# Router matmul as three rounded passes, with PSUM-bank alignment, routing totals and a few early and late steps rearranged

## The reference

```
h = rmsnorm(xn) * scale                       # 8192 tokens x 128
q, k, v = h @ wq, h @ wk, h @ wv              # 16 heads of 64
attn = softmax(q k^T / 8) v @ w_out + b_out   # per sequence of 512, fp32
z = silu(xn @ rw1 + rb1) @ rw2 + rb2          # router: 128 -> 512 -> 8
top 2 of 8 experts, softmax over the two
moe = sum_e weight_e * (silu(xn @ w1[e] + b1[e]) @ w2[e] + b2[e])
out = x + attn + moe
```

## Time and profile before

| what | value |
|---|---|
| median of 3 runs | 1897.01 us (1896.87 to 1897.79) |
| the profiled execution | 1897.01 us, span 1895.1 us |
| TensorE clock granted | 0.996 of full |
| PE busy | 1835.2 us (97%) |
| VectorE busy | 1625.8 us (86%) |
| ScalarE busy | 1198.8 us (63%) |
| chain that ended last | PE 55%, ACT 21%, DVE 14%, issue 8%, SPq 1%, DMA 1% |

### The profile page before, as it was taken

The page is one execution under the profiler, slowest core; times in us unless marked ns, Lnnn a source line. Parts: engine busy times, 40 slices in busy tenths (PEclk is TensorE's granted clock), DMA queues, the critical chain, the costliest instruction groups (busy, mean ns, idle before and its releaser), DMA issues.

```text
span 1895.1 us, 74351 instructions
## 1 busy us (share of the span) xinstructions
PE 1835.2 (97%) x32434; PEld 1149.5 (61%) x32434; DVE 1625.8 (86%) x2297; ACT 1198.8 (63%) x2969; POOL 711.9 (38%) x623
## 2 busy tenths in 40 slices
PE   8999999999999999998899999999999999999997
PEld 5555555555555555555566666666666666666655
DVE  5999999999999999989788888888888888888885
ACT  6666766666666666664567575666666666666563
POOL 3244654434444445432023234324324333333152
PEclk9999999999999999999999999999999999999999
DMA  3133322111111111111434434333333333333342
GB/s 90 27 82 109 97 94 57 42 48 37 47 38 47 48 48 48 29 42 44 116 74 78 90 72 89 78 84 77 90 72 65 93 69 84 72 83 78 78 76 53
DMA packets 154485, 130.13 MB, mean 69 GB/s; under 512 B 27664, under 2 KB 139024, under 8 KB 154128
## 3 DMA queue, kind: packets, MB, share of 16 engines
q1 hardware_dynamic: 123568, 104.65, 20.1%
q0 software_dynamic: 30592, 20.73, 8.3%
HBM read 93.15 MB, written 34.27 MB: 67 GB/s over the span
## 4 chain that ended last, share of the span: by engine, by line
PE 55%; ACT 21%; DVE 14%; issue 8%; SPq 1%; DMA 1%; ACTq 0%; DVEq 0%
PE pair L329 15%; ACT PR L910 13%; PE pair L310 12%; PE pair L469 7%; DVE NM L551 6%; PE pair L342 4%; PE pair L295 4%; DVE PT L559 3%; ACT ZT L992 3%; PE pair L385 3%; ACT ZZ L995 3%; PE pair L283 3%; PE pair L271 2%; DVE OT L568 2%; PE pair L239 1%
## 5 line engine op out<-in xcount | busy, mean ns | idle before, releaser
L910 ACT ACTIVATE PR<-pair,NM 128x512 f32<-128x512 f32 x1024 | 694.3, 696 | 544.1 <-DVE NM L551 543.7
L559 DVE STREAM_TRANSPOSE PT<-PR 128x1024 f32<-128x1024 f32 x512 | 631.7, 1240 | 109.5 <-ACT PR L910 96.3
L551 DVE TENSOR_REDUCE NM<-pair 128x2 f32<-128x1024 f32 x512 | 598.9, 1210 | 26.9 <-PE pair L310 26.6
L310 PE MATMUL pair<-KS,QS 64*32 64x512 f32 x8192 | 502.6, 596 | 18.1 <-ACT KS L886 10.2
L329 PE MATMUL pair<-PT,V 32*64 32x256 f32 x16384 | 479.4, 378 | 11.8 <-ACT ZZ L995 9.6
L1151 POOL DMA_INDIRECT out<-YS,IDW x156 | 248.9, 1596 | 611.3 <-DVE YS L828 387.5
L329 PEld LDWEIGHTS pair<-PT,V 32*64 32x64 f32 x16384 | 375.5, 131 | 165.5 <-issue 111.8
L310 PEld LDWEIGHTS pair<-KS,QS 64*32 64x32 f32 x8192 | 124.6, 106 | 259.2 <-issue 164.9
L910 ACT ACTIVATION_READ_ACCUMULATOR PR<-pair,NM 128x1 f32 x1024 | 218.3, 213 | 0.0
L992 ACT ACTIVATE ZT<-pair,BT 128x512 f32<-128x512 f32 x156 | 109.6, 703 | 115.4 <-PE pair L224 115.3
L1098 POOL TENSOR_TENSOR TH<-TH,HS 128x512 f32<-128x512 f32 x64 | 82.0, 1280 | 227.8 <-ACT HS L948 227.8
(11 more groups left out here) (121 smaller groups left out, 1688.3 us busy)
## 6 DMA issues: line engine op xcount, KB each, us to landing
RB<-l_rows SPq DMA_DIRECT2D x128, 256.0 KB, 4.4
E<-w_tab SPq DMA_DIRECT2D x39, 512.0 KB, 4.6
XG<-slots SPq DMA_DIRECT2D x39, 264.0 KB, 4.2
E<-in_w SPq DMA_DIRECT2D x39, 256.0 KB, 3.7
xin<-in_x SPq DMA_DIRECT2D x16, 256.0 KB, 3.0
XQ<-in_x SPq DMA_DIRECT2D x16, 256.0 KB, 3.2
l_rows<-RT SPq DMA_DIRECT2D x256, 2.0 KB
w_tab<-SPL SPq DMA_DIRECT2D x8, 512.0 KB, 2.7
```

Of the source, the lines that this page charges most:

```text
L310: m = pe.do.matmul(bank[2 * (s % 2) + r][32 * c:32 * c + 32, :], QS[rows, u % 2, c, at:at + 32], KS[rows, g % 2, c, :], start=True, stop=T ...
L551: dve.do.tensor_reduce(NM[:, step % 4], pairs[s % 2][:], AX.X, ALU.max, negate=True).then_inc(sem["dve_max"])
L559: dve.do.transpose(PT[:].rearrange("p c k q -> p (c k) q")[:, :, 32 * slot:32 * slot + 32], PR[:, step % PRB].rearrange("p r k -> p (r k)" ...
L910: act.do.activation(PR[:, step % PRB, r, :], bank[2 * (s % 2) + r], ACT.Exp, bias=NM[:, step % 4, r:r + 1], accum_out=RS[:, g % 2, r, at:a ...
```

## The change

1. The router's first layer: XT and R1 become pairs of fp32r tiles (high and low part). `router` calls `three` in place of one fp32 matmul. ScalarE writes the high part of XT; a new VectorE instruction, `split_x`, subtracts it from the bank to give the low part. It stands at the start of G = 8r, behind `denominators` and ahead of the first maximum. The bank of the transposed tokens now comes free with `split_x`, not with ScalarE's copy. At the start ScalarE and GpSimd split rw1 once, from a staging place in `acc`.
2. The tokens of sequence 0 are transposed before the loop, ahead of the first scores.
3. `ring.align` is removed.
4. `ends`, `starts` and `rows_of_tiles` follow `totals` directly at G = 131.
5. The denominators of the last unit are done at G = 256 like the others at their unit's end, behind VectorE's work for the last expert tile.
6. GpSimd no longer waits for VectorE's first rows before it starts on the routed rows of sequence 0.

```
-    def align(self):
-        self.used += -self.used % GH
...
             def turn_x(r):
-                free[bk] = sem["act_xTs"], r + 1
+                free[bk] = sem["dve_xTs"], r + 1
...
             def attending(G):
-                if k == 2:
-                    ring.align()
...
             def router(r, c):
+                w = [R1[:, k, c * P:(c + 1) * P] for k in range(2)]
+                m = [XT[:, k, :] for k in range(2)]
+                pe.wait_ge(sem["dve_xTs"], r + 1)
-                pe.do.matmul(bank[bk], R1[:, c * P:(c + 1) * P], XT[:], start=True, stop=True).then_inc(sem["pe_r1"])
+                three(pe, bank[bk], w, m).then_inc(sem["pe_r1"])
...
+            def split_x(r):
+                dve.wait_ge(sem["act_xTs"], r + 1)
+                dve.wait_ge(sem["pe_r1"], NC * r)
+                dve.do.tensor_tensor(XT[:, 1, :], bank[BANK["xT", r]], XT[:, 0, :], ALU.subtract).then_inc(sem["dve_xTs"])
...
             def between(G):
-                if G == EARLY * GB + 4:
-                    ends()
-                if G == EARLY * GB + 5:
-                    starts()
-                if G == EARLY * GB + 6:
-                    rows_of_tiles()
...
+            split_x(0)
             for G in range(TIMES + 8):
-                if k == 0 and 0 < u < UNITS:
+                if k == 0 and 0 < u <= UNITS:
                     denominators(u - 1)
+                turned(G)
...
-                if G == TIMES - 1:
-                    denominators(u)
                 experts(G)
...
+            def weight_high(name, src, dst, c, scale):
+                act.do.mul(dst[:, 0, s], src[:, s], scale).then_inc(sem["act_whi"])
+            weight_high("r1", r1_s, R1, 0, 1.0)
+            turn_x(0)
...
+            def weight_low_part(src, dst, c, rank):
+                pool.do.tensor_tensor(dst[:, 1, s], src[:, s], dst[:, 0, s], ALU.subtract).then_inc(sem["pool_wlo"])
-            pool.wait_ge(sem["dve_hc"], QT)
             routed_rows(0)
+            weight_low_part(r1_s, R1, 0, 1)
```

More of the change, by code:

```diff
@@ L41 @@
     pe_w2
[L42 removed]
+    dve_junk dve_one dve_ri0 dve_ones dve_bn dve_mv dve_var dve_hc dve_xTs dve_max dve_tr
     dve_OT dve_ri dve_rt dve_acc dve_sum dve_gate dve_pm dve_at dve_pk dve_row dve_to dve_wt dve_tot
     dve_xl dve_s dve_y dve_ys dve_rb1h dve_pm0 dve_hf
[L45 to L46 removed]
+    act_whi act_xTs act_V act_k act_q act_exp act_th act_hz act_tanh act_shi act_xh act_lgs act_zt act_zz
+    pool_half pool_pow pool_wlo pool_slo pool_hc pool_hr pool_xc pool_xr pool_tok pool_spare pool_tz pool_hs pool_bhalf
     pool_pad0 pool_pad pool_TOK pool_idw
@@ L147, in block_kernel @@
             XR = sb("XR", [P, 3, 2, QT, ROW], F32, routing)
-            XT = sb("XT", [P, S], F32, routing)
-            R1 = sb("R1", [P, HID], F32, routing)
+            XT = sb("XT", [P, 2, S], F32R, routing)
+            R1 = sb("R1", [P, 2, HID], F32R, routing)
             R2 = sb("R2", [P, NC, 32], F32, routing)
@@ L178, in block_kernel @@
         ov = out[0:T].rearrange("(b t p) d -> b p t d", t=QT, p=P)
+        r1_s = acc[:].rearrange("p t d -> p (t d)")
         full = [P, QT, D]
@@ L186, in x_in, with weight_low @@
             return sem[f"x_{b % 3}"], 16 * (b // 3 + 1)
+        def weight_low(name, c):
+            return sem["pool_wlo"], 1
         def place_of(g, s):
@@ L590, in project_out @@
                     dve.wait_ge(sem["pe_oT"], b)
+                    dve.wait_ge(sem["pool_wlo"], 1)
                     dve.do.tensor_scalar(dst, ps, BO[:], None, ALU.add).then_inc(sem["dve_acc"])
@@ L725, in place, with turned @@
                 dve.do.tensor_copy(junk[:, 2:3], junk[:, 0:1]).then_inc(sem["dve_gate"])
+            def turned(G):
+                r, h = divmod(G, 8)
+                if h == 0 and 0 < r < NB:
+                    split_x(r)
             def between(G):
@@ L760, in route @@
                     best(r)
-            lane = slice(0, 1)
-            nt, end, beg, cnt = (tot[:, k] for k in range(4))
-            ex, st, j = (tix[:, k] for k in range(3))
-            cmp = tic[:]
-            wide_e = [1, NT, E]
-            def totals():
+            def totals():
+                lane = slice(0, 1)
+                nt, end, beg, cnt = (tot[:, k] for k in range(4))
+                i = TILES[lane, :]
+                ex, st, j = (tix[:, k] for k in range(3))
+                cmp = tic[:]
+                wide_e = [1, NT, E]
                 dve.wait_ge(sem["pe_cnt"], 1)
                 dve.do.tensor_copy(cnt, bank[BANK[("cnt",)]][lane, 0:E]).then_inc(sem["dve_tot"])
-            def ends():
                 dve.wait_ge(sem["dve_tot"], 1)
@@ L782, in ends @@
                 dve.do.tensor_tensor_scan(end, ONES[lane, 0:E], nt, 0.0, ALU.mult, ALU.add).then_inc(sem["dve_tot"])
-            def starts():
-                i = TILES[lane, :]
                 dve.wait_ge(sem["dve_tot"], 6)
@@ L880, in _ @@
             act = Engine(eng)
+            def weight_high(name, src, dst, c, scale):
+                s = slice(c * 512, (c + 1) * 512)
+                act.wait_ge(sem[f"load_{name}{c}"], 16)
+                act.do.mul(dst[:, 0, s], src[:, s], scale).then_inc(sem["act_whi"])
             def keys(g, c):
@@ L896, in turn_x @@
                 act.wait_ge(sem["pe_r1"], NC * r)
-                act.do.copy(XT[:], bank[BANK["xT", r]]).then_inc(sem["act_xTs"])
+                act.do.copy(XT[:, 0, :], bank[BANK["xT", r]]).then_inc(sem["act_xTs"])
             def probs(g, s):
@@ L1036, in power @@
                 pool.do.tensor_tensor(sqo[:, r], sqi[:], HALF[:], ALU.pow).then_inc(sem["pool_pow"])
+            def weight_low_part(src, dst, c, rank):
+                s = slice(c * 512, (c + 1) * 512)
+                pool.wait_ge(sem["act_whi"], rank)
+                pool.do.tensor_tensor(dst[:, 1, s], src[:, s], dst[:, 0, s], ALU.subtract).then_inc(sem["pool_wlo"])
             def attention_rows(b):
@@ L1339, in _ @@
                 load(f"wv{c}", WV[:, cols], wv[:, cols])
-            load("r10", R1[:], rw1)
+            load("r10", r1_s, rw1)
             load_q(1)
```

13 lines of the change are left out of this document (2 added, 11 removed).

## The result

| | median | lowest to highest | ratio |
|---|---|---|---|
| before | 1896.91 us (5 runs) | 1894.68 to 1897.79 | |
| after | 1916.79 us (5 runs) | 1914.57 to 1919.28 | 1.0106, interval 1.0092 to 1.0121 |

The change costs 19.9 us. The prediction was 1901.2 with a range up to 1908.5: its sign was right, its size was a fifth of the truth, and the range did not hold the time. The profiled execution of the changed kernel took 1913.43 us, 16.4 us more than that of the kernel before; the traces hold that much of the 19.9 us.

What follows compares the result with a forecast made beforehand. TensorE and VectorE were both nearly full in the first half, TensorE set the second. First half +3.1, ring +4.0, boundary -4.3, start +0.6, tail +0.3 sum to +3.7: 1900.7 us, named 1901.2, range 1893 to 1908.5.

Steps and rivals of the forecast that it cites:

- How much of it shortens the span is limited by VectorE in stretch A: Router blocks: TensorE's saving of 0.34 us a pair counts up to VectorE's waits for scores, 5.9 us gained.
- stretch A: About 18 us around the router in each round of 8 G, where TensorE was said to set the pace.
- the second kind: Router places at G%16 = 10, 11, claimed to gain 0.51 us each, 8 times.
- the first kind: Router places at G%16 = 2, 3, claimed to gain at most 0.46 us each, booked 4 times.
- Split: New VectorE instruction ahead of a round's first maximum: 0.60 us paid in each of 15 rounds, +9.0 us.
- the bank rival: Bank held by the split delays weighted and later scores; a round costs 1.1 us, 1908.5 us in all; chance 0.20.
- Ring without alignment: Second half: queries wait for the second take-out in 11 units at 0.36 us each, +4.0 us.
- in B there is room: First half away from the router: TensorE has 0.4 us to spare, so missing alignment costs nothing there.
- Start: Before the first maximum: VectorE's split of sequence 0 adds +0.6 us (0 to 1.5); GpSimd's earlier start adds nothing.
- Boundary: Totals at G = 131: pads leave earlier, so unit 33's RB transfer comes 4.3 us earlier, -4.3 us.
- Tail: Last unit's reciprocals move 4.8 us later, RB still lands just in time: +0.3 us (0 to 4).
- Slower: Outcome above 1900.8 us for the whole kernel, given a chance of 0.54.

Runs made afterwards that it cites:

- e_nosplit: Kernel before with the router's first product in three passes, without the low half of x and without the VectorE split; 1892.3 us, 0.9988.
- e2_router: Kernel before with only the router's part of the change (three passes, VectorE split, sequence 0 transposed ahead of the loop); 1904.3 us, 1.0051.
- The pair of relief kernels: e_nosplit and the kernel before, each with ScalarE's router tanh on 128 of its 512 columns; 1887.05 us and 1894.61 us.
- e_nosplit_relief: e_nosplit with ScalarE's router tanh on 128 of its 512 columns; 1887.05 us, 0.9954 against the kernel before.
- e2_noalign: Kernel before without ring.align and nothing else of the change; 1903.96 us, 1.0045.
- e_poolwait: Kernel before without GpSimd's wait for VectorE ahead of the first routed rows, nothing else; 1897.52 us, 1.0013.
- e2_totals: Kernel before with only the totals, ends, starts and rows of tiles in one place at G = 131; 1893.34 us, 0.9985.
- e2_no_align_no_pool: Changed kernel with ring.align and GpSimd's wait put back; 1907.34 us, 1.0057 against the kernel before.
- e_denoms: Kernel before with only the last unit's denominators moved behind the last expert rows, on a 2043 us chip; 2044.26 us, 1.0005.
- e_totals: Kernel before with only the totals done in one piece at G = 131, on a 2043 us chip; 2036.36 us, 0.9974.

## Why the prediction was wrong, step by step

**The step that failed: "How much of it shortens the span is limited by VectorE in stretch A".** It gave 4 x 0.46 + 8 x 0.51 = 5.9 us. In e_nosplit, where nothing else of the change is in the way, the second kind gains 0.36 in seven units and the first kind nothing, 2.5 us; in e2_router it is 2.3. The limit that I had left out is ScalarE. After (timeline), where the earlier trace rows show before:

```profile
468.21 0.50 PE L223 MATMUL pair<-XT,R 128*128 128x512 f32 x1
...
469.34 0.75 ACT L947 ACTIVATE TH<-pair,RB1H 128x512 f32<-128x512 f32 x1
469.79 1.95 PE L311 MATMUL pair<-KS,QS 64*32 64x512 f32 x32
469.92 0.75 ACT L950 ACTIVATE HS<-pair,RB 128x512 f32<-128x512 f32 x1
470.49 0.76 ACT L947 ACTIVATE TH<-pair,RB1H 128x512 f32<-128x512 f32 x1
470.99 2.36 DVE L556 TENSOR_REDUCE NM<-pair 128x2 f32<-128x1024 f32 x2
471.06 0.76 ACT L950 ACTIVATE HS<-pair,RB 128x512 f32<-128x512 f32 x1
471.92 3.71 PE L330 MATMUL pair<-PT,V 32*64 32x256 f32 x128 [0.18 <-issue]
...
476.76 2.35 DVE L556 TENSOR_REDUCE NM<-pair 128x2 f32<-128x1024 f32 x2 [0.45 <-PE pair L311]
```

and before, the end of the same piece of work:

```profile
461.10 0.73 ACT L948 ACTIVATE HS<-pair,RB 128x512 f32<-128x512 f32 x1
...
462.00 3.71 PE L329 MATMUL pair<-PT,V 32*64 32x256 f32 x128
```

The pair of router blocks takes 469.79 - 468.21 = 1.58 us: predicted 1.57. The scores come 0.33 us earlier as hoped and the first maximum no longer waits. But ScalarE takes four pieces of 0.75 us out of the two blocks one behind the other, and the last ends at 471.82, as long after the pair's start as before (461.83 - 458.21 = 3.62, and 3.61 now). `weighted` needs that bank. It starts 2.13 us behind the scores in place of 1.88, so the second maximum's wait grows from 0.19 to 0.45: the gain is handed on from one wait to the next. VectorE's waits were an upper bound, and I took the bound for the gain without asking what else ended at the same moment. The pair of relief kernels shows it: the gain returns when ScalarE is faster, and only then.

**Split: +9.0 us, right.** In e2_router the take-outs step by 0.59 to 0.66 in the twelve rounds without another event. It stands where predicted, with the maximum right behind it, and `weighted` idles 1.12 us where I had said 1.1. After, answering to the earlier trace rows:

```profile
550.06 0.65 DVE L549 TENSOR_TENSOR XT<-pair,XT 128x512 fp32r<-128x512 f32 x1
550.62 2.35 DVE L556 TENSOR_REDUCE NM<-pair 128x2 f32<-128x1024 f32 x2
550.86 4.24 PE L330 MATMUL pair<-PT,V 32*64 32x256 f32 x128 [1.12 <-DVE XT L549]
556.22 2.36 DVE L556 TENSOR_REDUCE NM<-pair 128x2 f32<-128x1024 f32 x2 [0.29 <-PE pair L311]
```

Here `weighted` also took 4.24 us in place of 3.71; the maximum behind it waited 0.29 us, and this round's step is 1.00 in place of 0.60. The same meeting, larger, is in e2_router at G = 18:

```profile
123.30 3.63 PE L333 MATMUL pair<-PT,V 32*64 32x256 f32 x115 [1.12 <-DVE XT L554]
127.25 0.68 PE L333 MATMUL pair<-PT,V 32*64 32x256 f32 x13 [0.32 <-issue]
...
129.06 2.36 DVE L561 TENSOR_REDUCE NM<-pair 128x2 f32<-128x1024 f32 x2 [0.68 <-PE pair L314]
```

That is the bank rival, and it decides only where a slow `weighted` adds to the delay: in the other rounds of these two traces the second maximum behind the split waits 0.1 us at most.

**Not in the sum at all: VectorE's small instructions beside GpSimd's long ones, 2.9 us of the router alone.** The jump at G = 34, after (timeline):

```profile
238.70 2.41 DVE L675 SCALAR_TENSOR_TENSOR gt<-gt,CON 128x32 f32<-128x32 f32 x1
238.77 1.28 POOL L1143 TENSOR_TENSOR SPL<-RAW,SPL 128x512 fp32r<-128x512 f32 x1
240.01 1.04 POOL L1051 TENSOR_TENSOR HR<-xin,mv 128x512 f32<-128x512 f32 x1
```

An instruction that takes 0.17 us in other rounds lasts as long as GpSimd's two. Its like is in e2_router (2.53), and in e_nosplit_relief (2.54 at 233.93), which has no split. In e_nosplit the two engines meet 0.8 us apart and it takes 0.17:

```profile
233.45 0.17 DVE L680 SCALAR_TENSOR_TENSOR gt<-gt,CON 128x32 f32<-128x32 f32 x1
234.23 1.29 POOL L1162 TENSOR_TENSOR SPL<-RAW,SPL 128x512 fp32r<-128x512 f32 x1
```

So it is a matter of phase, not of the router's work: any edit that shifts the engines by under a microsecond can draw again. Of VectorE's instructions, before has 2.3 us of such excess, after 6.7, e2_router 6.0. The Trainium skill, page "SBUF — State Buffer", section "Who interferes with whom", has the mechanism: VectorE with two operands in SBUF and GpSimd share a read port that one of them holds alone. The trace agrees (2.41 us against 0.17; the instruction has two such operands). Instructions with one tensor operand were slow beside GpSimd as well: the copy at G = 30 and the four tensor_scalar at the start.

With this the router alone is accounted for, by the steps of its take-outs: 0.1 at the start, 15 x 0.60 = 9.0 for the splits, 2.0 and 0.9 for two collisions, 0.8 at G = 18, most of it the 0.68 us behind the slow `weighted`, -2.3 in six of the eight units of the second kind and +0.7 in the two others. These two had their own events, a take-out that waited 0.82 us for RB (G = 30) and a maximum that waited 0.94 us behind a `weighted` of 4.35 us (G = 62). That is 11.2, and its take-out at G = 130 is 11.3 us late.

**Ring without alignment: +4.0 in the second half, right; 0 in the first half alone, wrong.** In before the queries never wait for the take-out there. In after they do in nine units, 0.28 or 0.39 us each; one of them, and the group of them all (930 to 1870 us; busy, mean ns, idle before and its releaser):

```profile
1091.09 1.25 DVE L573 TENSOR_TENSOR OT<-pair,RB 128x512 f32<-128x512 f32 x2
1092.40 1.78 PE L296 MATMUL pair<-HF,WQ 128*128 128x256 f32 x7 [0.39 <-DVE OT L573]
```

```profile
L296 PE MATMUL pair<-HF,WQ 128*128 128x256 f32 x232 | 57.3, 390 | 2.8 <-DVE OT L573 2.8
```

The take-outs behind them step by 0.3 to 0.5, 3.5 us in all (14.4 at G = 254 against 10.9 at 146). I had counted eleven units at 0.36. That the two agree is a little luck, since kernels that keep the alignment drift by up to 2.2 us over the same stretch. In the first half the queries wait for the take-outs 9.8 us in before and 14.5 in e2_noalign. The same group of the two, up to 930 us, before and then e2_noalign:

```profile
L295 PE MATMUL pair<-HF,WQ 128*128 128x256 f32 x288 | 72.8, 396 | 9.8 <-DVE OT L568 9.8
```

```profile
L295 PE MATMUL pair<-HF,WQ 128*128 128x256 f32 x288 | 72.0, 393 | 14.5 <-DVE OT L566 14.4
```

I had argued that "in B there is room". There is not: the queries wait already, and 0.6 us more of waiting is not all slack. It costs at most some 3 of the 4.2 us of e2_noalign at G = 130; 0.94 is the meeting with GpSimd at G = 30. In the changed kernel the first half loses only about 2 us by it (14.2 at G = 130 against 11.7 with `align` put back, of which 0.5 is the start), and most of these are again the step at G = 30. That the split makes VectorE later than TensorE anyway would explain the rest; it wasn't tested.

**Start: +0.6 predicted, 1.5 measured, and not for the reason given.** I had written of GpSimd's earlier start "nothing". After, the first 12 us:

```profile
7.96 1.03 POOL L1065 TENSOR_TENSOR XR<-XQ,mv 128x512 f32<-128x512 f32 x1
7.97 3.60 DVE L535 TENSOR_SCALAR HR<-xin,mv,sqo 128x128 f32<-128x128 f32 x4 [1.88 <-POOL sqo L1038]
9.07 1.04 POOL L1068 TENSOR_TENSOR XR<-XR,sqo 128x512 f32<-128x512 f32 x1
...
11.62 0.66 PE L240 MATMUL pair<-idn,HR 128*128 128x128 f32 x4 [1.16 <-DVE HR L535]
```

The wait that was removed had kept the two engines apart. The four tensor_scalar on VectorE take 3.60 us, in before 1.12. The transposition starts at 11.62, in before at 10.51; e_poolwait, which has only this, is 1.55 us late at its first take-out, e2_router, which has the router's new start and keeps the wait, 0.12. (Kernels at 1896 us that keep the wait lie between -0.7 and +0.9 there.)

**Boundary: -4.3 predicted.** The take-out of unit 33 no longer waits for RB, and the bunched instructions cost 2.6 us at G = 134 which I had put at nothing: in after 2.6 - 4.9 - 1.0 = -3.2 us over G = 134 to 142. They hold up the maximum, ScalarE waits for it and TensorE for ScalarE; the clock fell to 0.50 at 902.6 for 3.4 us, and the `weighted` of that place took 4.52 us. After, answering to the earlier trace rows:

```profile
901.16 1.09 PE L311 MATMUL pair<-KS,QS 64*32 64x512 f32 x16 [3.09 <-ACT PR L912]
...
922.24 0.21 DVE L586 STREAM_TRANSPOSE RT<-RI 128x32 f32<-128x32 f32 x1
922.48 2.36 SPq L1220 DMA_DIRECT2D l_rows<-RT  x4
926.56 1.86 SPq L1225 DMA_DIRECT2D RB<-l_rows  x2
...
933.77 1.25 DVE L573 TENSOR_TENSOR OT<-pair,RB 128x512 f32<-128x512 f32 x2
```

The row sums now leave 0.03 us after they are ready, before 4.4. The step is right in its mechanism; its price, by e2_totals, is -2.8 us (-4.5 to -1.1).

**Tail: +0.3 predicted, the wait right, its size too small and its consequence missed.** After, answering to the earlier trace rows:

```profile
1891.79 0.24 DVE L582 RECIPROCAL RI<-RS 128x16 f32<-128x16 f32 x1
...
1896.46 1.25 SPq L1225 DMA_DIRECT2D RB<-l_rows  x2
...
1901.85 1.29 DVE L573 TENSOR_TENSOR OT<-pair,RB 128x512 f32<-128x512 f32 x2 [9.57 <-DMA RB<-l_rows]
...
1903.20 3.44 PE L343 MATMUL pair<-OT,WO 128*128 128x256 f32 x8 [4.75 <-DVE OT L573]
```

and TensorE at the start of that last row (window, us, busy, granted clock, DMA share, GB/s):

```profile
1903.20:1905.00 1.80, 1.80 (x4) 0.50 0.48 138
```

RB's second half was issued 4.67 + 0.63 = 5.30 us behind the reciprocals (I took 3.8), and the take-out came 4.76 us behind that (I took up to 4.2). The prediction had named a last take-out that waits for RB by more than 1 us as a sign that it is wrong. TensorE, idle for 4.75 us, then took 3.44 us for eight matmuls, 1.99 in e2_router: its granted clock was 0.50, where the prediction had no term for the clock. From the take-out of G = 254 to the end it is 39.1 us in after and 40.5 in e2_no_align_no_pool, the two kernels with the move at 1896 us, and 35.5 to 37.4 in the eight without it. So in the traces the move costs between 1.8 and 5 us. e_denoms alone, +1 us with zero inside its interval, has the waits without the lower clock.

**The chances.** Slower had 0.54 and came true. The range was too narrow: it was made of the bounds of terms that I had. Of the missing 16 us, the failed step holds about 3.5 (5.9 against 2.3 to 2.5) and had no bound on its far side. The collisions had no term at all; the ring in the first half outside of stretch A, the wait of GpSimd and the bunched instructions were put at nothing, and the tail was mis-sized.

## What to carry to other kernels

A wait that disappears is worth only the distance to the next thing that would have ended the same step: before a saving is booked, list every releaser of each instruction behind it and when each ends, and move them one by one. A wait that looks useless may keep two engines apart on a shared port; a removed one, or any small shift, can redraw such collisions, so a term for them belongs in the range. And a gain read at one place of one trace is checked against traces of other kernels that leave the place alone.

## What the runs showed of the hardware that was not expected

- The same kernel before takes 1896 us on two chips and 2043 on two others. On the latter the first half has a stretch of granted clock 0.50 in nearly every round; in e_totals it stands behind one in which TensorE was busy for 1.3 of 3 us.
- A VectorE instruction on 128 x 32 elements takes 0.17 us alone and 2.41 beside two GpSimd instructions of 1.28 and 1.04 us; four tensor_scalar of 128 x 128 take 3.60 us in place of 1.12.
- Three fp32r matmuls in place of one in fp32 save 17% of the pair's time, 1.58 us against 1.91.
- The last projection, eight matmuls behind 4.75 us of an idle TensorE, took 3.44 us at a granted clock of 0.50 and 1.99 us at 1.00.
- `weighted` takes 3.9 to 4.6 us in place of 3.71 in five to nine of its 128 times in a trace at 1896 us, at a granted clock of 1.00, in the kernel before as well. Its cause stayed open.
